# Attention on one core: which of two waits ACT's exponential carries, and which stands alone in front of it

## Chip, cores and metric

One core of a Trainium2 chip. The metric is the device time of one execution in microseconds, the median of several runs. TensorE is called PE here, VectorE DVE, ScalarE ACT, GpSimd POOL; SP issues the DMAs.

## What is computed

Two transformer layers over 4096 tokens of width 256, in fp32. Each layer has attention with 16 heads of 16 columns, then a feed-forward part, with residuals and layer norms. Layer 0 is causal; layer 1 is not. The part that the change touches, cut from the reference:

```python
# layer 0
scores = jnp.einsum('bhqd,bhkd->bhqk', q, k) / jnp.sqrt(jnp.float32(HEAD_DIM))
causal = jnp.tril(jnp.ones((t, t), dtype=bool))
scores = jnp.where(causal[None, None], scores, -jnp.inf)
attn = jax.nn.softmax(scores, axis=-1)
out = jnp.einsum('bhqk,bhkd->bhqd', attn, v)
# layer 1: the same without the mask
weights = jax.nn.softmax(scores, axis=-1)
out = jnp.einsum('bhqk,bhkd->bhqd', weights, V)
```

## The kernel before

The program runs in stages with a barrier between them: projections of layer 0, attention of layer 0, feed-forward, projections of layer 1, attention of layer 1, output projection, and a last network. Only `attention` matters here; it is called for both layers.

**Tiling.** The 16 heads are four groups of four (`GH = 4`). A unit is one group and one block of 512 queries (`QB`), so there are 32 units in a layer. In a unit the keys run in tiles of 128: always 32 tiles in layer 1, and 32, 28, 24, ... 4 in layer 0, whose units of a group go from the last block of queries to the first. That makes 1024 key tiles in layer 1 and 576 in layer 0, 1600 in all. A key tile has four score matmuls, one a head: 128 keys by 512 queries each.

**The order of work.** `order(u)` writes out a list of steps for each unit, and PE, ACT and DVE each walk through the same list and take their own part of each step:

- `score`: PE multiplies K and Q into one of three PSUM banks (line 839), ACT takes the exponential of that bank into `att_probs` (line 898). The bank is then free.
- `max`: PE makes scores of the next unit (line 801) in one of two pairs of banks, DVE reduces them to maxima (line 915). The maxima are needed before the next unit starts. One such item stands behind every second score where there are enough of them; the last unit of a layer has none.
- `values`: PE multiplies `att_probs` of a key tile by V (line 864), in two halves of 256 queries, two key tiles behind the scores (`LAG = 2`). Each half has one matmul a head, four in all in different columns of the array.
- once a unit: `turn_max` (the maxima of the next unit turned, copied at line 879 and put into Q by a DMA), `keep_out` (line 908) and `turn_out` (PE at line 873, ACT's copy at line 903, then DVE's division at lines 952 and 956).

In a row, a key tile on PE is: score of head 0, of head 1, a maxima item, values (first half), score of head 2, of head 3, a maxima item, values (second half). PE waits for nothing but what its next instruction needs, but takes its queue in order.

**The waits.** `scored` is counted up by PE once a `score`, `turn_max` or `turn_out` (the steps in `RING`), `emptied` by ACT when it has read the bank. Both count in the order of the ring, so PE's score number n waits until the exponential of number n-3 has ended. `values_done` is counted up by PE after the second half of a key tile's values. `att_probs` has room for four key tiles (`PBUFS = 4`), so the exponential of head 0 of tile k waits for the values of tile k-4; for heads 1 to 3 of a tile only the score is waited for. `out_read` is DVE's, one a unit, and the copy at line 903 waits for it beside `scored`.

**Two waits in front of one instruction.** An instruction of these engines carries one wait here. Where `wait_ge` is called twice ahead of an instruction, the built program has the wait that was called first on the instruction itself, and the one called last in an EVENT_SEMAPHORE instruction of its own in front of it, on ACT's queue (named with the line of its `wait_ge`). It takes its place in the order: what is behind it isn't looked at before it is met. In the kernel before, that is line 894, the wait for `scored`.

Of the kernel before, what the change touches and what calls it, by code (L numbers as in the profile page):

```python
# [533 lines left out]
def attention(nc, core, ps, ident, layer, causal, q_parts, k_parts, v_dram, K, o_all):  # L534
# [51 lines left out]
    def order(u):  # L586
        nk, nxt, todo = keys(u), u + 1, hosted[u]
        slots = nk * GH
        last = max([n for n, (w, _) in enumerate(todo) if w == nxt], default=-1)
        near_end = slots - (SEAM if nk > QT else SEAM - 2)  # L590
        cost = [max_width(*item) + 64 for item in todo]
# [47 lines left out]
    def width(u, kt):  # L639
        return max(0, kt - (keys(u) - QT)) * P if causal else 0  # L640

    plan = [order(u) for u in range(UNITS)]
    RING = ("score", "turn_max", "turn_out")
# [20 lines left out]
    def column(h):  # L664
        b, j = half_of(h)
        return b * PAIRS + j

    with ExitStack() as ctx:
# [21 lines left out]
        scored = core.sem(pre + "scored")  # L690
# [15 lines left out]
        with nc.Block() as block:  # L706
            if causal:
                @block.gpsimd
                def _(pool):
                    pool.memset(band[:], 0.0).then_inc(ones_set, 1)  # L710
                    pool.memset(pick[:], 0.0).then_inc(ones_set, 1)
                    pool.wait_ge(ones_set, 2)
                    for b in range(2):
                        rows = slice(b * HALF, (b + 1) * HALF)
                        for m in range(2):

                            pool.affine_select(out=pick[rows, m], in_=pick[rows, m], compare_op=ALU.not_equal, fill=1.0,
                                               base=m * HALF, pattern=[[-1, P]], channel_multiplier=1).then_inc(ones_set, 1)
                            pool.affine_select(out=band[rows, m], in_=band[rows, m], compare_op=ALU.is_ge, fill=MASKED,
                                               base=m * HALF, pattern=[[-1, P]], channel_multiplier=1).then_inc(ones_set, 1)  # L720
                    pool.wait_ge(ones_set, 10)
                    for u in range(UNITS):
                        for kt in range(keys(u) - QT, keys(u)):
                            pool.wait_ge(emptied, last_score(u, kt) + 4)
                            square = probs[:, (n_key[u] + kt) % PBUFS, :, width(u, kt):width(u, kt) + P]
                            pool.affine_select(out=square, in_=square, compare_op=ALU.is_ge, fill=0.0, base=0,  # L726
                                               pattern=[[0, GH], [1, P]], channel_multiplier=-1).then_inc(masked, 1)
# [60 lines left out]
            def _(pe):  # L788
# [36 lines left out]
                for u in range(UNITS):  # L825
# [4 lines left out]
                    for step, at in zip(plan[u], place[u]):  # L830
                        what = step[0]
                        if what in RING:
                            pe.wait_ge(emptied, at + 1)
                        if what == "score":
                            _, kt, h = step
                            b, j = half_of(h)
                            lo = width(u, kt)
# [38 lines left out]
            @block.scalar  # L876
            def _(act):
                def keep_turned(par, at):
                    act.activation(negT[:, par, :], ring(at)[0:PARTS * NEG, 0:P], ACT.Copy).then_inc(emptied, 1)  # L879

                act.sem_inc(emptied, 2)
                act.sem_inc(out_kept, 1)
                act.wait_ge(scored, 1)
                keep_turned(0, -1)
                for u in range(UNITS):
                    for step, at in zip(plan[u], place[u]):
                        what = step[0]
                        if what == "score" and step[2] == 0:

                            act.wait_ge(values_done, n_key[u] + step[1] + 1)  # L890
                        if what == "turn_out":
                            act.wait_ge(out_read, step[1] + 1)
                        if what in RING:
                            act.wait_ge(scored, at + 2)
                        if what == "score":
                            _, kt, h = step
                            lo = width(u, kt)
                            act.activation(probs[:, (n_key[u] + kt) % PBUFS, column(h), lo:QB], ring(at)[:, lo:QB], ACT.Exp,  # L898
                                           scale=SCALE).then_inc(emptied, 1)
                        elif what == "turn_max":  # L900
                            keep_turned((u + 1) % 2, at)
                        elif what == "turn_out":
                            act.activation(out[:].rearrange("p t h e -> p (t h e)"), ring(at), ACT.Copy).then_inc(emptied, 1)  # L903
                        elif what == "keep_out":
                            v = step[1]
                            act.wait_ge(values_done, n_key[v + 1] + PBUFS)

                            act.activation(outT[:], ps[:, 6, :], ACT.Copy).then_inc(out_kept, 1)
# [897 lines left out]
```

## Time and profile before

| | |
|---|---|
| median of 3 runs | 5400.65 us (5383.06 to 5416.19) |
| the profiled execution's own time | 5378.21 us |
| its span, first to last instruction | 5375.6 us |
| instructions | 101793 |
| mean granted TensorE clock | 0.941 |
| layer 0's exponentials, first and last start | 284.4 and 1833.3 us |
| layer 1's exponentials, first and last start | 2520.5 and 5093.0 us |

The profile is one execution. Its engine rows count an instruction as busy from its start to its end; a matmul's end is modelled, and a matmul can begin while the one before it is still in the array, so that PE's busy share says little about what it could still take. In the timeline a row merges instructions of one kind that follow each other: start, time from the first's start to the last's end, count, and in brackets how long the engine had been idle and what ended that. PEld is PE's weight load, which runs beside the matmuls.

### The profile page before, as it was taken

Reading aid. Unit: us, or ns where it says so; the run is one execution under the profiler, and the core shown is the slowest. Engines: PE = TensorE matmul, PEld = TensorE weight load, DVE = VectorE, ACT = ScalarE, POOL = GpSimd, SP = SyncE. Lnnn points to the kernel's source line nnn. Section 1 sums busy time; section 2 is a strip of 40 time slices with the busy share of each in tenths; the row PEclk is TensorE's granted clock in tenths of the full one; section 3 lists DMA queues with packets and bytes.
Section 4 is the critical chain, followed back from the end, with each engine's and each line's share of the span. In section 5 each row is a group of like instructions: output and inputs, shape, how many; then the busy total and the mean of one; then the engine's idle time right before and its main releaser. Section 6 shows DMA issues by size and latency. Waiting matters only on the chain. (4 is left out here: it accounts for less than half of the span.)

```text
span 5375.6 us, 101793 instructions
## 1 busy us (share of the span) xinstructions
PE 5017.1 (93%) x42036; PEld 2053.1 (38%) x42036; DVE 4509.5 (84%) x5080; ACT 3777.9 (70%) x7189; POOL 316.1 (6%) x482
## 2 busy tenths in 40 slices
PE   7699999999999678876999999999999999999998
PEld 4333433433333245542333333333333333333343
DVE  3678889889876479948999999999999999999356
ACT  2177788788777422232888888888888888888853
POOL 3200000000000011130000000000000000000030
PEclk7589999999998789995999999999999999999999
DMA  4301010010000000052100001000010000000000
GB/s 130 105 22 27 11 30 20 14 39 11 11 7 7 20 16 12 6 182 55 42 4 8 5 5 42 8 5 5 5 42 8 5 4 8 8 5 5 9 1 32
DMA packets 138201, 131.30 MB, mean 24 GB/s; under 512 B 61802, under 2 KB 96490, under 8 KB 137706
## 3 DMA queue, kind: packets, MB, share of 16 engines
q1 hardware_dynamic: 137738, 124.80, 8.2%
q8 instruction: 331, 5.42, 0.4%
q14 instruction: 132, 1.08, 0.1%
HBM read 76.75 MB, written 46.66 MB: 23 GB/s over the span
## 5 line engine op out<-in xcount | busy, mean ns | idle before, releaser
L915 DVE TENSOR_REDUCE att_mx<-ps 128x2 f32<-128x1024 f32 (+2 forms) x3200 | 3757.9, 1192 | 304.4 <-PE ps L801 205.2
L898 ACT ACTIVATE att_probs<-ps 128x512 f32<-128x512 f32 (+3 forms) x6400 | 3386.3, 583 | 648.2 <-PE ps L839 559.8
L864 PE MATMUL ps<-att_probs,att_V 128*17 128x256 f32 (+1 forms) x25088 | 1970.5, 389 | 0.2
L839 PE MATMUL ps<-att_Q,K 50*128 50x512 f32 (+3 forms) x6400 | 1732.5, 495 | 49.9 <-ACT att_probs L898 28.8
L801 PE MATMUL ps<-K,att_Q 48*128 48x512 f32 (+2 forms) x6400 | 1429.0, 415 | 91.3 <-DVE att_mx L915 54.9
L839 PEld LDWEIGHTS ps<-att_Q,K 50*128 50x128 f32 x6400 | 686.8, 186 | 1417.0 <-ACT att_probs L898 1262.9
L864 PEld LDWEIGHTS ps<-att_probs,att_V 128*17 128x17 f32 x25088 | 426.2, 96 | 1071.5 <-issue 605.9
L801 PEld LDWEIGHTS ps<-K,att_Q 48*128 48x128 f32 x6400 | 679.6, 194 | 173.2 <-DVE att_mx L915 121.9
L726 POOL TENSOR_SCALAR_AFFINE_SELECT att_probs<-att_probs 128x512 f32<-128x512 f32 x128 | 81.6, 637 | 1551.4 <-ACT att_probs L898 1551.4
L1169 PE MATMUL ps<-wguT,mlp_xqT 128*128 128x512 f32 (+1 forms) x384 | 161.5, 571 | 0.5 <-DVE mlp_h L1277 0.2
L1368 POOL MEMSET mix_power<- 128x1 f32 x1 | 0.1, 99 | 2682.3 <-POOLq L131 2682.3
L952 DVE RECIPROCAL att_rden<-att_out 128x16 f32<-128x16 f32 x64 | 16.2, 254 | 161.3 <-ACT att_out L903 161.3
L879 ACT ACTIVATE att_negT<-ps 32x128 fp32r<-32x128 f32 x64 | 16.1, 251 | 184.4 <-PE ps L811 184.4
L1208 ACT ACTIVATE mlp_gate<-ps 128x704 f32<-128x704 f32 x32 | 24.2, 757 | 141.6 <-PE ps L1169 141.6
L483 DVE TENSOR_TENSOR proj_qprod<-ps,proj_tabT 128x1024 f32<-128x1024 f32 x32 | 38.4, 1220 | 83.5 <-PE ps L329 83.5
L1169 PEld LDWEIGHTS ps<-wguT,mlp_xqT 128*128 128x128 f32 x384 | 72.6, 196 | 73.9 <-issue 65.3
L1187 PE MATMUL ps<-wdT,mlp_hqT 128*128 128x256 f32 (+1 forms) x384 | 96.0, 392 | 1.1 <-DVE mlp_y L1256 1.1
L1607 PE MATMUL ps<-xT_all,net_w 128*128 128x512 f32 x192 | 95.1, 618 | 0.0
L392 ACT ACTIVATE proj_xT<-ps 128x512 f32<-128x512 f32 x32 | 17.6, 595 | 109.9 <-PE ps L311 109.9
L1555 DVE TENSOR_SCALAR cn_cf<-cn_th,cn_ab 128x512 f32<-128x512 f32 x24 | 13.1, 546 | 83.6 <-ACT cn_th L1689 83.0
L1187 PEld LDWEIGHTS ps<-wdT,mlp_hqT 128*128 128x128 f32 (+1 forms) x384 | 71.2, 192 | 27.2 <-issue 12.4
L791 PE MATMUL ps<-att_band,att_pick 64*128 64x128 bf16 x1024 | 81.5, 228 | 0.0
(207 smaller groups left out, 2385.6 us busy)
## 6 DMA issues: line engine op xcount, KB each, us to landing
att_Q<-qhi_scratch SPq DMA_DIRECT2D x256, 64.0 KB, 2.3
K<-khi_scratch SPq DMA_DIRECT2D x256, 64.0 KB, 2.3
v_scratch<-proj_vpad SPq DMA_DIRECT2D x16, 544.0 KB, 3.4
att_V<-v_scratch SPq DMA_DIRECT2D x64, 136.0 KB, 2.5
att_Q<-qlo_scratch SPq DMA_DIRECT2D x128, 64.0 KB, 2.3
K<-klo_scratch SPq DMA_DIRECT2D x128, 64.0 KB, 2.3
proj_x<-in_L_attn_x SPq DMA_DIRECT2D x8, 512.0 KB, 5.1
qhi_scratch<-proj_qhipart SPq DMA_DIRECT2D x16, 256.0 KB, 3.0
```

What stands on the lines that cost most here:

```text
L483: dve.tensor_tensor(prod[name][:, m], of[name], tabT[:, j % 2, m, :].unsqueeze(1).to_broadcast([P, 2, B]), ALU.mult).then_inc(prods[name], 1)
L726: pool.affine_select(out=square, in_=square, compare_op=ALU.is_ge, fill=0.0, base=0, pattern=[[0, GH], [1, P]], channel_multiplier=-1).the ...
L791: return pe.matmul(dst, pick[rows, m], band[rows, m], start=False, stop=(m == 1))
L801: mm = pe.matmul(bank(b)[:, 0:wide], Q[rows, slot_of(u), j, qt * P:(qt + 1) * P], K[rows, par_of(u), j, c * QB:c * QB + wide], start=True, ...
L839: mm = pe.matmul(ring(at)[:, lo:QB], K[rows, par_of(u), j, kt * P:(kt + 1) * P], Q[rows, slot_of(u), j, lo:QB], start=True, stop=True)
L864: mm = pe.matmul(ps[VW * h:VW * h + HV, 6, lo:(part + 1) * (QB // 2)], V[:, par_of(v), kt, HV * h:HV * (h + 1)], probs[:, (n_key[v] + kt) ...
L898: act.activation(probs[:, (n_key[u] + kt) % PBUFS, column(h), lo:QB], ring(at)[:, lo:QB], ACT.Exp, scale=SCALE).then_inc(emptied, 1)
L915: dve.tensor_reduce(mx[:, min(u % NQB, 1), :, j, qt, c], ps[:, 2 + 2 * pair:4 + 2 * pair, 0:max_width(u, i) // 2], AX.X, ALU.max).then_inc ...
L1169: mm = pe.matmul(gu_ps[:, b:to], xqT[:, par, c, :], wguT[:, c, b:to], start=(c == 0), stop=(c == DC - 1))
L1187: mm = pe.matmul(down, hqT[0:kw, par, k, :], wdT[0:kw, k, :], start=(k == 0), stop=(k == NK - 1))
L1208: act.activation(gate[:], gate_ps, ACT.Silu).then_inc(s["gate_kept"], 1)
L1607: mm = pe.matmul(bank1(k, m), nets.w1[:, c, m * P:(m + 1) * P], xT_all[:, c, cols_of(k)], start=(c == 0), stop=(c == DC - 1))
```

## The change

In ACT's walk through the steps, the wait for `scored` is called ahead of the waits for `values_done` and `out_read`, not behind them.

```diff
@@ -885,13 +885,13 @@
                 for u in range(UNITS):
                     for step, at in zip(plan[u], place[u]):
                         what = step[0]
+                        if what in RING:
+                            act.wait_ge(scored, at + 2)
                         if what == "score" and step[2] == 0:
 
                             act.wait_ge(values_done, n_key[u] + step[1] + 1)
                         if what == "turn_out":
                             act.wait_ge(out_read, step[1] + 1)
-                        if what in RING:
-                            act.wait_ge(scored, at + 2)
                         if what == "score":
                             _, kt, h = step
                             lo = width(u, kt)
```

What the built programs have on ACT at the end of a unit and the start of the next, in layer 0, before. A row is one kind of instruction in a row; in brackets are the semaphores it waits for, in order, the last of two being the one that it carries. Semaphores are used again from stage to stage and are printed by their first name: `proj0_q_lo_made` is `scored`, `proj0_q_hi_stored` is `values_done`, `proj0_k_lo_stored` is `out_read`.

```order
L898 ACTIVATE att_probs<-ps 128x512 [waits proj0_q_lo_made,proj0_q_hi_stored]
L898 ACTIVATE att_probs<-ps 128x512 [waits proj0_q_lo_made] x3
L898 ACTIVATE att_probs<-ps 128x512 [waits proj0_q_lo_made,proj0_q_hi_stored]
L908 ACTIVATE att_outT<-ps 128x512 [waits proj0_q_hi_stored]
L898 ACTIVATE att_probs<-ps 128x512 [waits proj0_q_lo_made] x3
L898 ACTIVATE att_probs<-ps 128x512 [waits proj0_q_lo_made,proj0_q_hi_stored]
L898 ACTIVATE att_probs<-ps 128x512 [waits proj0_q_lo_made] x3
L903 ACTIVATE att_out<-ps 128x512 [waits proj0_q_lo_made,proj0_k_lo_stored]
L898 ACTIVATE att_probs<-ps 128x512 [waits proj0_q_lo_made,proj0_q_hi_stored]
```

And the same place after, on ACT:

```order
L898 ACTIVATE att_probs<-ps 128x512 [waits proj0_q_hi_stored,proj0_q_lo_made]
L908 ACTIVATE att_outT<-ps 128x512 [waits proj0_q_hi_stored]
L898 ACTIVATE att_probs<-ps 128x512 [waits proj0_q_lo_made] x3
L898 ACTIVATE att_probs<-ps 128x512 [waits proj0_q_hi_stored,proj0_q_lo_made]
L898 ACTIVATE att_probs<-ps 128x512 [waits proj0_q_lo_made] x3
L903 ACTIVATE att_out<-ps 128x512 [waits proj0_k_lo_stored,proj0_q_lo_made]
L898 ACTIVATE att_probs<-ps 128x512 [waits proj0_q_hi_stored,proj0_q_lo_made]
```

No activation has moved. In the rows with two waits, one in four exponentials and the copy at line 903, the two have changed places. The orders of PE, DVE, POOL and SP are the same in both programs.

## Rows read from the trace of the kernel before

**Rows 1.** The page: span, busy us, share and instructions of each engine.

```profile
span 5375.6 us, 101793 instructions
...
PE 5017.1 (93%) x42036; PEld 2053.1 (38%) x42036; DVE 4509.5 (84%) x5080; ACT 3777.9 (70%) x7189; POOL 316.1 (6%) x482
```

**Rows 2.** Busy us (instructions) of PE, PEld, DVE, ACT, POOL by stretch, then clock.

```profile
400.00:1600.00 1200.00, 1164.89 (x11342) 466.25 (x11343) 1023.41 (x1021) 935.50 (x1880) 63.71 (x100) 0.97 0.07 19
2575.00:5015.00 2440.00, 2431.80 (x23396) 888.25 (x23396) 2389.06 (x2089) 2135.93 (x3965) 0.00 (x0) 1.00 0.04 12
5020.00:5093.00 73.00, 72.34 (x652) 26.80 (x648) 0.68 (x2) 67.37 (x131) 0.00 (x0) 1.00 0.01 1
```

**Rows 3.** Who waited for whom, whole run: us, times, longest.

```profile
ACT att_probs L898 <- PE ps L839: 559.8, 1693, 4.9
```

**Rows 4.** Timeline, layer 1: start, length, engine, line, count, [idle before].

```profile
4000.49 0.63 PE L864 MATMUL ps<-att_probs,att_V 128*17 128x256 f32 x8
...
4001.05 0.50 PE L839 MATMUL ps<-att_Q,K 50*128 50x512 f32 x2
...
4001.64 2.25 ACT L898 ACTIVATE att_probs<-ps 128x512 f32<-128x512 f32 x4 [0.22 <-PE ps L839]
...
4001.72 0.63 PE L864 MATMUL ps<-att_probs,att_V 128*17 128x256 f32 x8
...
4002.27 0.52 PE L839 MATMUL ps<-att_Q,K 50*128 50x512 f32 x2
...
4003.52 0.50 PE L839 MATMUL ps<-att_Q,K 50*128 50x512 f32 x2
...
4004.11 2.25 ACT L898 ACTIVATE att_probs<-ps 128x512 f32<-128x512 f32 x4 [0.22 <-PE ps L839]
```

**Rows 5.** Groups by line, 2700 to 4300: count, busy us, mean ns, idle.

```profile
L915 DVE TENSOR_REDUCE att_mx<-ps 128x2 f32<-128x1024 f32 x1273 | 1546.9, 1225 | 17.0 <-PE ps L801 8.7
L898 ACT ACTIVATE att_probs<-ps 128x512 f32<-128x512 f32 x2543 | 1383.5, 596 | 191.8 <-PE ps L839 148.1
```

**Rows 6.** Line 894 (durations min/median/max in ns).

```profile
L894 ACTq EVENT_SEMAPHORE  x1664: 17/17/17, 284.3 to 5096.5; - x185
```

**Rows 7.** Timeline, layer 0, around two pairs of scores.

```profile
1003.88 0.50 PE L839 MATMUL ps<-att_Q,K 50*128 50x512 f32 x2
...
1004.47 1.09 ACT L898 ACTIVATE att_probs<-ps 128x512 f32<-128x512 f32 x2 [0.32 <-PE ps L839]
...
1005.23 0.50 PE L839 MATMUL ps<-att_Q,K 50*128 50x512 f32 x2
...
1005.77 1.09 ACT L898 ACTIVATE att_probs<-ps 128x512 f32<-128x512 f32 x2 [0.21 <-PE ps L839]
```

**Rows 8.** Timeline of ACT, layer 0, the copy at line 903.

```profile
902.60 0.60 ACT L903 ACTIVATE att_out<-ps 128x512 f32<-128x512 f32 x1 [0.39 <-PE ps L873]
903.09 1.08 ACT L898 ACTIVATE att_probs<-ps 128x512 f32<-128x512 f32 x2
```

**Rows 9.** Timeline of PE, layer 1, first and last small slip.

```profile
2533.96 0.51 PE L839 MATMUL ps<-att_Q,K 50*128 50x512 f32 x2
...
5012.00 0.52 PE L839 MATMUL ps<-att_Q,K 50*128 50x512 f32 x2
```

**Rows 10.** Timeline, layer 1's last unit.

```profile
5062.05 0.49 PE L839 MATMUL ps<-att_Q,K 50*128 50x512 f32 x2
...
5062.64 2.06 ACT L898 ACTIVATE att_probs<-ps 128x512 f32<-128x512 f32 x4 [0.16 <-PE ps L839]
...
5063.03 0.75 PE L839 MATMUL ps<-att_Q,K 50*128 50x512 f32 x2
```

**Rows 11.** Timeline of PE, layer 0.

```profile
303.73 0.75 PE L839 MATMUL ps<-att_Q,K 50*128 50x512 f32 x2
...
1746.19 0.52 PE L839 MATMUL ps<-att_Q,K 50*128 50x512 f32 x2
```

**Rows 12.** Timeline of DVE, layer 0.

```profile
593.53 18.62 DVE L915 TENSOR_REDUCE att_mx<-ps 128x2 f32<-128x1024 f32 x16
```

## The prediction

> **What bounds the kernel now.** The page's first lines come first [rows 1]: PE 93% busy, DVE 84%, ACT 70%. These are averages over stages, so the second view is busy time by stretch [rows 2]. Layer 1's attention without its last unit (2575 to 5015) has PE at 2432 of 2440 us, DVE at 2389 (98%) and ACT at 2136 (88%); its last unit (5020 to 5093) has PE at 72.3 of 73, ACT at 67.4 and DVE at nothing; layer 0's attention (400 to 1600) has PE at 97%, DVE at 85% and ACT at 78%. By shares, DVE and PE could both be the bound of layer 1. Third, the longest waits [rows 3]: the exponentials wait for the score matmuls (559.8 us, 1693 times). A busy PE can hide lost time, because the ends of its matmuls are modelled and overlap, so the last view is the order in time.
>
> Layer 1 repeats one pattern [rows 4]. Call the score matmuls of one key tile s0 to s3 and their exponentials e0 to e3. PE issues s0 and s1 together (4001.05), two maxima matmuls, eight value matmuls (4001.72), then s2 and s3 (4002.27), maxima, values, and s0 again at 4003.52. From s0 to s2 it takes 1.22 us, from s2 to the next s0 1.25 us. The difference is in one place: the pair s0, s1 lasts 0.50 us, so both start together, while s2, s3 lasts 0.52, so s3 starts about 0.02 late. Scores go through a ring of three banks, so s3 needs e0's bank: e0 starts at 4001.64 and takes 0.60 [rows 4, 5], ends at 4002.24, and s3 starts at 4002.27 + 0.02 = 4002.29, some 0.05 after it. Everything behind s3 on PE's in-order queue is then 0.02 late. s1 waits in the same way for e2, but is not late.
>
> **Why e0 is late.** L894's wait for the scores stands as an instruction of its own in front of 1664 activations (1600 e0 and 64 copies at L903), each taking 17 ns [rows 6]. In time order [rows 7], from the start of the scores to the start of the exponential takes 0.59 us for e0 (1003.88 to 1004.47; in rows 4, 4001.05 to 4001.64; in rows 10, 5062.05 to 5062.64), but 0.54 for e2, which carries its wait (1005.23 to 1005.77). So the handover through a separate instruction costs 0.05 to 0.06 us. That this instruction costs nothing while ACT works is seen where e0 follows the L903 copy [rows 8]: 902.60 and 903.09 are 0.49 apart with the copy 0.60 long, as between e0 and e1 in rows 7 (two in 1.09).
>
> **The change, part by part.** It moves no work: PE, DVE, POOL and SP keep their order, and ACT has as many instructions. On e0 it swaps the two waits: the separate one is now for the value matmuls, four tiles back, and e0 carries the one for its score.
>
> (1) The separate wait. What it waits for is the second half of the values of tile k-4, which PE issues in tile k-2: for the tile whose s0 starts at 4003.52 that is the group at 4000.49, over by 4001.12 [rows 4]. e0 of that tile starts at 4004.11, and e3 in front of it is the last quarter of the block at 4001.64. So the wait has long been met when ACT gets to it, and e3's 0.60 us covers the instruction; 0.22 us of idle time follow even then. Cost taken: nothing. If the cover failed, it would be the 0.06 us of today, paid on the other wait. Queued behind the wait are e0 to e3 and, through the ring, s3.
>
> (2) e0 starts 0.055 us sooner after its score. Bounds for one tile: 0 (PE has other work) and 0.06 (everything behind is released by e0). In layer 1 the saving is cut at 0.02, because s3 then meets the values in front of it, not e0. s1 behind e2 is not late even now; with the change both halves look like s0's, 1.22 each.
>
> (3) The copy at L903 carries its score wait too. It comes once a unit; the e0 behind it moves with it, and that is in the count below.
>
> Count by tiles, from the pair s2, s3 and the end of e0, over all 1600 tiles. Where s3 starts 0.05 us after e0's end it waits for e0.
> - Layer 1, 31 units of 32 tiles: 887 tiles slip by 0.02 to 0.03 (first at 2533.96, last at 5012.00 [rows 9]): 887 x 0.02 = 18 us. 73 slip by more than 0.06 (unit starts, slots without a maxima item): 73 x 0.055 = 4 us. The other 32 do not wait for e0.
> - Last unit, 32 tiles without maxima [rows 10]: the pair s2, s3 lasts 0.75, a slip of 0.26. The circle is e0, s3, values, s0, e0, with nothing beside it on PE, and all 0.055 come out of it: 32 x 0.055 = 2 us.
> - Layer 0, 576 tiles: 221 have the small slip (last pair at 1746.19 [rows 11]): 221 x 0.02 = 4 us. 153 have one over 0.06, the first of those with a steady pattern at 303.73 (0.75 for the pair [rows 11]): 153 x 0.055 = 8 us. In 202 s3 does not wait for e0: nothing.
>
> Sum: 18 + 4 + 2 + 4 + 8 = 36 us. The least by these rows is 0; the most is 1600 x 0.06 = 96 us, if no tile were cut at 0.02. I take 36, since the steady 1.22 of the half tile that waits for nothing stands in all of layer 1.
>
> **Is DVE the floor?** It matters: two reductions are in each layer-1 tile, 2 x 1.225 = 2.45 us [rows 5] of 2.46 to 2.47 (4001.64 to 4004.11 in rows 4). But in layer 0, sixteen of them stand in 18.62 us [rows 12], so (18.62 - 1.22) / 15 = 1.16 us apart, at 1.22 each: a reduction starts before the last one has ended. Two in a tile need 2.32, and DVE has 0.14 to spare. The idle time that DVE is given in layer 1 is put down to PE [rows 5]. The Trainium skill, "VectorE: DVE Perf Modes", section "The DRAIN you can't avoid", says that the next operation does not start until the pipe is empty, with an exception for operations that are not held; by its first half layer 1 would have almost no room, and the trace does not agree for these reductions (1.16 against 1.22).
>
> **Against the runs shown.** The profiled execution took 5378.21 us (span 5375.6): 5378.2 - 36 = 5342 on its own scale. The median of the runs is 5400.65, 22 higher and spread over 33 us; the same 36 us off it gives 5364.
>
> **Rivals.**
> A. DVE sets layer 1's period after all. Then the 18 us fall away, since a shorter PE pattern only makes PE wait for the reductions: 4 + 2 + 4 + 8 = 18 us off, 5383. For it: 98% busy. Against it: rows 12. Chance 0.12. By the page's rule the room would be 0.01 to 0.02 a tile, 9 to 18 us of the 18.
> B. More than the slip comes back: PE's 1.22 is not a floor in layer 1, or in layer 0 e0's lead goes on to reductions and masks in the units that end with idle PE. If every second tile gave 0.055 and not its slip, 1600 / 2 x 0.055 = 44 us, plus half of the 36: about 62 us, 5339. For it: ACT's 559.8 us of waiting [rows 3] is far above what I count. Against: most of it lies beside a PE that works. Chance 0.12.
> C. The change does nothing that shows: e0 starts at 0.59 whatever carries the wait, because it is the first after idle time. 5401. Against: e2 too starts after idle time, at 0.54 (rows 7: 0.21 idle). Chance 0.06.
> D. Slower: the values are what comes last. If e0 was released by the value matmuls, then the instruction that carried that wait was right before, and now ACT's queue stands at it and pays 0.055 after it, with e0 to e3 and PE's ring behind: by the same count +36 us, 5437, and at most +96. It decides from the point where the values of tile k-4 end after s0 of tile k, which is 3 us later than now. The time order puts the values' end 3 us ahead of e0 (part 1), and rows 3 put the exponentials' waits on the scores' line L839. Chance 0.03.
> The forecast, with its sum within 25 to 48 us: 0.67.
>
> **How the numbers follow.** What a measurement of this kernel can tell from no change is about 1%, 54 us. The forecast's 36 us is 0.67%. Of its 0.67 I put 0.05 over 1% for the spread of the runs, of B 0.09: 0.14 faster. Slower by over 1% needs the upper half of D or a disturbed median: 0.03. The rest, 0.83, is within 1%. The range: 5335 (B) to 5393 (A with 10 us of the runs' spread) leaves out C, D and B's far end.
>
> **What would show it.** Right: L894's instruction is gone, one at the values' wait is in its place, 1600 + 64 as before; from s0 to e0 0.53 to 0.54 us; the pair s2, s3 at 0.50 in layer 1, its tile at 2.44 to 2.45, that stretch of rows 2 shorter by 20 us or so; DVE's share up to 99% with no longer reductions; in the last unit the pair s2, s3 at 0.69 or 0.70. Wrong: e0 still at 0.59 (C); e0 at 0.54 with the tile at 2.46 (A; then s0 to s2 grows and maxima matmuls wait for att_mx); exponentials whose wait ends with L864 (D). A granted clock in layer 0 away from the 0.97 of now [rows 2] would move the time for another reason: PE there falls to its lower level (1.2 GHz) in short stretches, and each 0.01 of clock over 1200 us is worth up to 12 us.

## The result: 57 us less, 1.04%, and the profile after

The changed kernel took 5319.25 us in the median (5309.70 to 5358.00), the kernel before, measured beside it, 5376.36 (5369.45 to 5416.19). The ratio is 0.9896, with an interval of 0.9874 to 0.9917. The forecast was 36 us off 5400.65, a ratio of 0.9933; what came is 57 us, and 5319 lies below the range's low end of 5335. Part of that distance is the starting value: the kernel before ran 24 us lower in this comparison than in the three runs that the prediction had. The ratio itself, put on 5400.65, gives 5344. But the interval does not hold the forecast's 0.9933, so something is missing from the sum. One of the seven executions of E5, an experiment below, took 7206 us at a granted clock of 0.55 and is left out of its figures.

The profiled execution took 5309.70 us. The page's head, against [rows 1]:

```profile
span 5307.5 us, 101793 instructions
...
PE 4955.1 (93%) x42036; PEld 2017.7 (38%) x42036; DVE 4498.3 (85%) x5080; ACT 3777.1 (71%) x7189; POOL 315.1 (6%) x482
```

As many instructions on each engine, 68 us less. PE's busy time fell by 62 us although it does the same matmuls. That does not tell the cause: a late second score makes a pair's busy time longer (0.52 for 0.50), and so does a lower clock. PE's mean granted clock is 0.948, against 0.941.

Where the 68 us are is seen in the exponentials' first and last start in each layer (line, engine, count, ns min/median/max, first and last start):

```profile
L898 ACT ACTIVATE att_probs<-ps x2304: 272/594/641, 283.9 to 1793.9; 128x512 f32<-128x512 f32 x160, 128x384 f32<-128x384 f32 x20, 128x256 f32<-128x256 f32 x12
...
L898 ACT ACTIVATE att_probs<-ps x4096: 591/597/634, 2478.3 to 5025.0; 128x512 f32<-128x512 f32 x196
```

Layer 0 went from 1548.9 us (284.4 to 1833.3) to 1510.0, 38.9 less where the forecast had 12. Layer 1 went from 2572.5 (2520.5 to 5093.0) to 2546.7, 25.8 less where it had 24. The other 3 us lie between and behind the layers. So layer 1 came as forecast and layer 0 gave three times as much.

Busy time by stretch, columns as in [rows 2]: layer 0's middle, layer 1 without its last unit, and layer 0 from first to last exponential.

```profile
400.00:1600.00 1200.00, 1167.05 (x11501) 465.71 (x11501) 1033.05 (x1034) 949.51 (x1907) 63.45 (x100) 0.98 0.07 19
2530.00:4950.00 2420.00, 2413.42 (x23418) 868.51 (x23414) 2383.16 (x2090) 2138.34 (x3969) 0.00 (x0) 1.00 0.04 12
283.90:1793.90 1510.00, 1466.82 (x14305) 586.37 (x14308) 1238.91 (x1241) 1190.59 (x2396) 80.59 (x127) 0.96 0.07 18
```

And the last of these in the kernel before:

```profile
284.40:1833.30 1548.90, 1503.27 (x14305) 600.70 (x14308) 1242.94 (x1241) 1192.13 (x2396) 80.93 (x127) 0.94 0.07 18
```

In layer 1 the clock is 1.00 in both, and the time fell with it unchanged: DVE's share rose from 97.9% to 98.5%, ACT's from 87.5% to 88.4%. In layer 0 the clock rose from 0.94 to 0.96 over the whole of it. The stretch that the prediction read (400 to 1600, 0.97 then and 0.98 now) leaves out the short units at the end, where much of the low clock lies.

**The handover.** The separate instructions have moved as the built programs said: 1600 at line 892 (the values), 64 at line 894 (out_read), 17 ns each, where [rows 6] had 1664 for the scores.

```profile
L892 ACTq EVENT_SEMAPHORE  x1600: 17/17/17, 278.7 to 5022.5; - x178
...
L894 ACTq EVENT_SEMAPHORE  x64: 17/17/17, 376.4 to 5027.0; - x64
...
ACT att_probs L898 <- PE ps L839: 284.5, 565, 4.9
```

The waits for the scores are down from 559.8 us in 1693 times [rows 3] to 284.5 in 565. That row overstates the change, because a stretch of idle time of 0.15 us or less is put down to nothing. All of ACT's idle time in front of its exponentials fell from 648.2 to 596.3 us on the two pages.

The same e0 as the one at 1004.47 in [rows 7], the 1081st exponential, now starts 0.53 us after its score instead of 0.59:

```profile
996.15 0.50 PE L839 MATMUL ps<-att_Q,K 50*128 50x512 f32 x2
996.68 1.09 ACT L898 ACTIVATE att_probs<-ps 128x512 f32<-128x512 f32 x2 [0.26 <-PE ps L839]
...
3899.72 0.50 PE L839 MATMUL ps<-att_Q,K 50*128 50x512 f32 x2
...
3900.94 0.50 PE L839 MATMUL ps<-att_Q,K 50*128 50x512 f32 x2
...
3902.17 0.50 PE L839 MATMUL ps<-att_Q,K 50*128 50x512 f32 x2
...
3909.50 0.49 PE L839 MATMUL ps<-att_Q,K 50*128 50x512 f32 x1
...
5001.30 0.57 PE L839 MATMUL ps<-att_Q,K 50*128 50x512 f32 x2
...
5002.35 0.63 PE L839 MATMUL ps<-att_Q,K 50*128 50x512 f32 x2
```

In layer 1 the pairs of scores now last 0.50, one each 1.22 us, and the tile takes 2.45 (3899.72 to 3902.17, against 2.47 in [rows 4]). Of the 992 pairs s2, s3 outside the last unit, 31 still have a small slip behind e0's bank and 34 a large one, where 887 and 73 had. In the last unit the pairs last 0.57 and 0.63 where one in two lasted 0.75 [rows 10].

**DVE is not the floor.** The groups of line 915 and 898, 2700 to 4300, against [rows 5]:

```profile
L915 DVE TENSOR_REDUCE att_mx<-ps 128x2 f32<-128x1024 f32 x1283 | 1553.7, 1225 | 9.4 <-PE ps L801 8.6
L898 ACT ACTIVATE att_probs<-ps 128x512 f32<-128x512 f32 x2565 | 1395.3, 596 | 180.4 <-PE ps L839 21.4
```

Ten more reductions fit into the same 1600 us, each as long as before, and DVE's idle time fell from 17.0 to 9.4 us. The 1283 reductions are busy for 1553.7 us together, 1211 ns for each at 1225 ns long, so they still overlap. From 3899.72 to 3909.50 in the timeline above are eight half tiles: 9.78 / 4 = 2.445 us a tile, just under two reductions of 1225 ns.

### The profile page after: what moved, and what is told of

Same layout as the page of the kernel before. It is cut to its first block and busy times, and to the rows that moved or that the text cites. A ratio compares the mean times of both kernels' runs of the same rounds, so it can differ in the third digit from the quotient of the medians.

```text
span 5307.5 us, 101793 instructions
## 1 busy us (share of the span) xinstructions
PE 4955.1 (93%) x42036; PEld 2017.7 (38%) x42036; DVE 4498.3 (85%) x5080; ACT 3777.1 (71%) x7189; POOL 315.1 (6%) x482
## 5 line engine op out<-in xcount | busy, mean ns | idle before, releaser
L898 ACT ACTIVATE att_probs<-ps 128x512 f32<-128x512 f32 (+3 forms) x6400 | 3385.5, 583 | 596.3 <-PE ps L839 284.5
L839 PE MATMUL ps<-att_Q,K 50*128 50x512 f32 (+3 forms) x6400 | 1686.9, 492 | 43.9 <-ACT att_probs L898 21.0
L801 PE MATMUL ps<-K,att_Q 48*128 48x512 f32 (+2 forms) x6400 | 1397.3, 414 | 91.7 <-DVE att_mx L915 54.7
L839 PEld LDWEIGHTS ps<-att_Q,K 50*128 50x128 f32 x6400 | 657.0, 185 | 1395.2 <-ACT att_probs L898 1269.7
L801 PEld LDWEIGHTS ps<-K,att_Q 48*128 48x128 f32 x6400 | 651.1, 192 | 173.6 <-DVE att_mx L915 122.1
```

The lines of the kernel that those rows point to most:

```text
L801: mm = pe.matmul(bank(b)[:, 0:wide], Q[rows, slot_of(u), j, qt * P:(qt + 1) * P], K[rows, par_of(u), j, c * QB:c * QB + wide], start=True, ...
L839: mm = pe.matmul(ring(at)[:, lo:QB], K[rows, par_of(u), j, kt * P:(kt + 1) * P], Q[rows, slot_of(u), j, lo:QB], start=True, stop=True)
```

## The experiments

Two questions. Which parts of the gain belong to which layer and which wait? And why did layer 0 give more than the count of late scores? One theory: the direct saving there is bigger than counted. The other: PE's clock fell to its lower level less often, because PE stands still less at the starts of units. All ratios are to the kernel before, run beside them.

### E1, the kernel before once more

No edit; it gives the scatter, and a second profile.

> The kernel before, unchanged, for the granted clock of each of its executions. The changed kernel's profile shows layer 0's attention 38 us shorter, where the prediction had 12. Theory C (clock): the rest is TensorE's granted clock there, so this kernel's executions scatter with their clock, 4 to 6 us for each 0.001, its mean clock is 0.940 to 0.942 against 0.946 for the changed one, and at the same clock the two kernels lie 35 to 45 us apart. Theory L (latency): the handover of 0.06 us comes back more often in layer 0 than counted; then at the same clock they lie 55 to 65 us apart and the clocks do not differ by more than 0.001.

Measured: 5393.72 us, ratio 1.0003 (0.9990 to 1.0016). Its runs' clocks lie between 0.936 and 0.942, and the time goes with them: a straight line through these 12 runs gives 3.7 us for each 0.001, one through all 61 runs of this kernel with the experiments 4.1; 3.9 is used below. (0.001 of clock over 5380 us is 10.8 us more at the lower of the two levels, half speed, so one such microsecond costs about 0.36.)

The expectation asked how far apart the two kernels lie at the same clock. By the line through the 61 runs, the 14 runs of the changed kernel (the nine above and E8) lie 45 us below it, 35 to 51 each. That is the upper end of theory C's 35 to 45, well under theory L's 55 to 65. Their mean clock is 0.9442, against 0.9404 in the 49 runs of the kernel before that stand beside the experiments; theory C had asked for 0.946.

The profile shows the clock's price in one unit. Layer 0 has units of 32 tiles; one of them, in E1:

```profile
1052.60:1140.70 88.10, 87.64 (x784) 33.51 (x783) 72.13 (x68) 68.08 (x132) 2.47 (x4) 0.90 0.02 6
...
1040.00:1048.00 8.00, 6.72 (x65) 3.43 (x69) 6.45 (x10) 5.27 (x14) 1.33 (x3) 0.94 0.06 18
...
1056.00:1064.00 8.00, 8.00 (x44) 3.29 (x40) 5.54 (x5) 4.63 (x9) 0.00 (x0) 0.50 0.02 8
```

and the same unit in the first profile of the kernel before:

```profile
1055.30:1136.70 81.40, 80.07 (x784) 31.07 (x783) 71.52 (x68) 67.89 (x132) 2.50 (x4) 1.00 0.02 6
...
1056.00:1064.00 8.00, 7.24 (x64) 3.10 (x64) 6.89 (x8) 7.10 (x15) 0.00 (x0) 1.00 0.17 49
```

The same 784 matmuls take 6.7 us longer. Its clock of 0.90 means 2 x 0.10 x 88.1 = 17.6 us at 1.2 GHz, so 0.38 us lost for each. In the eight microseconds at 0.50, PE is busy all the time and gets 44 matmuls done, not 64. What it did before the clock fell was the last tiles of the unit before, which get narrower down to 128 queries, with the turn of the maxima: PE is 84% busy there in E1 (6.72 of 8 us from 1040 to 1048). The clock fell at this turn of units in the first profile too:

```profile
1046.00:1054.00 8.00, 7.39 (x55) 3.47 (x59) 2.28 (x5) 4.12 (x12) 1.27 (x2) 0.50 0.02 5
```

There it was back at its upper level when the unit of 32 tiles began, at 1055.3. So both executions lost the clock at the same turn of units and got it back at different times.

### E2 and E3, the change in one layer only

```diff
+                        if causal and what in RING:        # E3: not causal
+                            act.wait_ge(scored, at + 2)
...
-                        if what in RING:
+                        if not causal and what in RING:    # E3: causal
                             act.wait_ge(scored, at + 2)
```

> The change in layer 0's attention alone. Both theories: layer 1's tile stays at 2.465 us. Theory C: 12 us from the handover and about 20 from the clock in layer 0, so 25 to 38 us faster than before, with a granted clock of 0.944 to 0.946. If the clock of the changed kernel's profile was luck and not the change: 10 to 15 us faster, clock 0.941. Theory L: 25 to 38 us faster with the clock of before.

> The change in layer 1's attention alone. By the steps of the prediction 24 us faster (22 us in 31 units, 2 us in the last one), the layer-1 tile at 2.445 us, layer 0 and its clock as before (0.940 to 0.942). If the clock rises through anything that shortens the program, this one rises too (0.944 or more) and it is 40 us or more faster.

Measured: E2 5363.74 us, ratio 0.9949 (0.9936 to 0.9961); E3 5370.13, ratio 0.9952 (0.9934 to 0.9971). The product is 0.9901, against 0.9896 for both together: the parts add up. The mean clock of the runs was 0.9436 in E2 and 0.9389 in E3, against 0.9395 in the kernel before beside them. So the clock goes up with the change in layer 0 and not with the change in layer 1, which saved as much time (25.8 us in the profile after). Set against the line of E1, E2 lies 12 us below it and E3 31, 43 together: of E2's gain over half came with the clock, of E3's nothing. Layer 0 from first to last exponential, E2:

```profile
284.70:1809.20 1524.50, 1482.79 (x14305) 592.15 (x14308) 1238.53 (x1241) 1190.51 (x2395) 80.59 (x127) 0.95 0.07 18
```

and E3:

```profile
288.40:1851.70 1563.30, 1517.57 (x14305) 605.80 (x14308) 1243.81 (x1241) 1191.50 (x2396) 80.60 (x127) 0.93 0.07 17
```

A single profile says little about the clock: E3 runs the same layer 0 as the kernel before and took 14 us longer in it. The means over the runs carry the comparison.

### E4, no separate wait for the values at all

Leaves out the wait for the value matmuls of four tiles ago; the wait for the score stays, and it covers that one, since PE makes those values before that score.

```diff
-                        if what == "score" and step[2] == 0:
-
-                            act.wait_ge(values_done, n_key[u] + step[1] + 1)
```

> The changed kernel without the separate wait for the value matmuls: PE issues the values of tile k-4 before the score of tile k, so the wait for the score covers it. It tells whether the separate instruction costs anything where it now stands. Prediction's part 1: nothing, within 3 us of the changed kernel (5310 to 5325), layer-1 tile 2.446. Rival: it still costs part of its 0.06 us in layer 0, where exponentials follow closely; then 5 to 15 us faster than the changed kernel.

Measured: 5322.56 us, ratio 0.9885 (0.9868 to 0.9903). The changed kernel gave 0.9896 (0.9874 to 0.9917), and 0.9893 (0.9873 to 0.9914) in E8. These intervals are some 10 us wide to each side, too wide for the rival's 5 to 15 us. At the same clock (the line of E1) E4 lies 44 us below the kernel before and the changed kernel 45. In 15 units of layer 0 that ran at full clock in E4 and in a profile of the changed handover (after, E2, E8), E4 is 0.3 us longer over 220 tiles, not shorter. So the separate instruction with a wait that has long been met costs nothing that shows.

### E5 and E6, more work for PE in layer 0's empty slots

In layer 0, one in two score pairs has no maxima item behind it in some tiles. E5 puts two matmuls there (K by K, results never read) in the kernel before, E6 in the changed one. They add 302 matmuls and take nothing away. (The expectation speaks of 174 places; there are 151.)

```diff
+                if causal and h % 2 and slot not in at:
+                    out.append(("fill", kt))
...
+                        if what == "fill":
+                            pe.wait_ge(max_taken, nxt + 1)
+                            for b in range(2):
...
+                                pe.matmul(ps[:, 2 + 2 * (nxt % 2) + b, :], K[rows, par_of(u), 0, 0:P],
+                                          K[rows, par_of(u), 0, 0:QB], start=True, stop=True)
```

> The kernel before, and in layer 0's attention, where no maxima item follows a pair of scores, one pair of matmuls of K with K into the free maxima banks, whose result nobody reads. The handover of 0.06 us stays as it is. It asks whether a fuller PE alone raises the granted clock. Theory C: yes, layer 0 spends fewer microseconds at the lower level (under 150 us, before 180), the clock is 0.943 or more and the time falls by 8 to 25 us, at 4 us for each 0.001. Theory L, or clock as luck: the clock stays at 0.939 to 0.940 and the time stays or rises by up to 10 us, as PE has 174 pairs more to do.

> The changed kernel with the same filler. Theory C: clock above that of the changed kernel (0.946 or more) and 0 to 15 us faster than it. Otherwise: clock the same, 0 to 10 us slower than it.

Measured: E5 5355.22 us, ratio 0.9951 (0.9931 to 0.9971); E6 5296.64, ratio 0.9836 (0.9814 to 0.9857). By the medians the filler is worth 31 us in both, E5 against the kernel before beside it (5386.66) and E6 against E8 (5327.97). By E5's ratio it is 26 us there, with an interval of 16 to 37. E6 is faster than both kernels. Layer 0 in E5:

```profile
284.10:1807.60 1523.50, 1484.94 (x14603) 594.18 (x14601) 1241.21 (x1241) 1196.19 (x2396) 80.85 (x127) 0.97 0.07 18
```

and in E6:

```profile
284.40:1780.30 1495.90, 1463.64 (x14603) 582.83 (x14601) 1236.56 (x1241) 1196.53 (x2395) 80.85 (x127) 0.98 0.07 18
```

E5 saves as much in layer 0 as E2 does (1523.5 and 1524.5 of 1548.9) with every e0 still late and 298 more PE instructions recorded. The runs' mean clock is 0.9502 in E5 and 0.9530 in E6, against 0.9402 and 0.9438 (E8) without the filler. Layer 0's time at the lower level, summed over stretches of 25 us as 2 x (1 - clock) x length, is 180 us before, 209 in E3, 149 in E2, 106 in the changed kernel, 78 in E5 and 51 in E6.

The filler's own time hardly shows at the place of [rows 11]. E6, where L849 makes the scores and L841 is the filler:

```profile
303.05 0.50 PE L849 MATMUL ps<-att_Q,K 50*128 50x512 f32 x2
303.38 0.40 PE L841 MATMUL ps<-K 48*128 48x512 f32 x2
...
304.27 0.50 PE L849 MATMUL ps<-att_Q,K 50*128 50x512 f32 x2
...
305.49 0.50 PE L849 MATMUL ps<-att_Q,K 50*128 50x512 f32 x2
```

The kernel before:

```profile
302.74 0.50 PE L839 MATMUL ps<-att_Q,K 50*128 50x512 f32 x2
...
305.20 0.49 PE L839 MATMUL ps<-att_Q,K 50*128 50x512 f32 x2
```

From the first pair to the third it is 2.44 us with the filler and 2.46 without, where E6 has the new handover too. Without the filler, the pair at 303.73 comes 0.23 sooner and its second score then waits for e0's bank.

Whole units tell more. Take the units of layer 0 that ran at full clock throughout, with the filler and without. In E5 they are 14, with 268 tiles and 60 of the 302 fillers: together 0.06 us shorter than in the kernel before (before, E1, E3). In E6 they are 19, with 300 tiles and 98 fillers: 1.9 us longer than with the changed handover alone (after, E2, E8). So, as far as these units show, the filler saves nothing where the clock is full, and its gain comes with the clock. By the line of E1 its matmuls also cost something: E5 lies 8 us above that line, and E6 40 us below it where the changed kernel lies 45, at clocks of 0.950 to 0.953 where the line (0.934 to 0.946) has no run of its own.

### E7 and E9, the separate wait at other exponentials

E7 is the kernel before, with a wait for the values also called ahead of e2's wait for its score, so that e2 too has its score's wait in an instruction of its own (the trace has 3264 of them at line 894, and 0.59 us from score to e2). E9 is the changed kernel with the old order at e2, and the new one left at e0. E7:

```diff
-                        if what == "score" and step[2] == 0:
+                        if what == "score" and step[2] in (0, 2):
```

and E9:

```diff
+                        if what == "score" and step[2] == 2:
+                            act.wait_ge(values_done, n_key[u] + step[1] + 1)
                         if what in RING:
```

> The kernel before with the suspected cost twice in a tile: e2 too carries a wait for the value matmuls (long met), and its score wait stands alone in front. By the steps of the prediction s1 then waits for e2 as s3 does for e0: 0.02 us more in each layer-1 tile (2.465 to 2.485), 17 to 22 us in layer 1; in layer 0 12 to 20 us, and by theory C some more through the clock. In all 25 to 60 us slower than before. If e0's lateness is not passed on through the ring, nothing.

> The changed kernel with the handover moved from e0 to e2: e0 carries its score wait, e2 carries the wait for the values and its score wait stands alone. E7 cost nothing, and the explanation to be tested is that a late s3 (by e0) and a late s1 (by e2) are the same 0.02 us: s3's slip pushes the next s0 and so gives s1 the time that a late e2 takes. Then the layer-1 tile here goes back to 2.465 us, with the slip now in the pair s0, s1, and this kernel is 17 to 22 us slower in layer 1 than the changed one, about 30 to 50 in all, some 10 to 25 us faster than before. If instead e2's lateness has no price at all, the tile stays at 2.446 and the time at the changed kernel's.

Measured: E7 5387.27 us, ratio 1.0001 (0.9984 to 1.0019); E9 5368.88, ratio 0.9972 (0.9954 to 0.9990). For E7 the expectation was wrong. Its timeline in layer 1:

```profile
4018.30 0.50 PE L839 MATMUL ps<-att_Q,K 50*128 50x512 f32 x2
...
4019.52 0.52 PE L839 MATMUL ps<-att_Q,K 50*128 50x512 f32 x2
...
4020.77 0.50 PE L839 MATMUL ps<-att_Q,K 50*128 50x512 f32 x2
...
4021.36 2.30 ACT L898 ACTIVATE att_probs<-ps 128x512 f32<-128x512 f32 x4 [0.16 <-PE ps L839]
...
4021.98 0.53 PE L839 MATMUL ps<-att_Q,K 50*128 50x512 f32 x2
```

Still one slip a tile. The reading: a late exponential frees its bank 0.59 + 0.60 + 0.05 = 1.24 us after its pair of scores began. Without a slip the next pair begins at 1.22, and its second score is 0.02 too early for the bank. But when one pair has slipped, PE is late with everything behind it, the next pair begins at 1.25 (4019.52 to 4020.77), and its second score finds the bank free. One late exponential or two, the tile is 0.02 longer. The whole of layer 1 fits this: outside the last unit, a small slip that waits for its bank stands in 540 second pairs and 388 first pairs of the 992 tiles, against 887 and none in the kernel before. The expectation had counted each handover as if it stood alone. E9's timeline shows the slip moved by half a tile:

```profile
4001.01 0.50 PE L839 MATMUL ps<-att_Q,K 50*128 50x512 f32 x2
...
4001.61 2.25 ACT L900 ACTIVATE att_probs<-ps 128x512 f32<-128x512 f32 x4 [0.23 <-PE ps L839]
...
4002.23 0.52 PE L839 MATMUL ps<-att_Q,K 50*128 50x512 f32 x2
...
4003.48 0.50 PE L839 MATMUL ps<-att_Q,K 50*128 50x512 f32 x2
```

Here 4001.01 is s2, s3 with e2 at 0.60, and the long pair is s0, s1. Tile: 2.47, as before the change; so layer 1's gain is gone (2571.3 us from first to last exponential, 2572.5 before). E9's layer 0:

```profile
283.70:1830.70 1547.00, 1507.09 (x14307) 603.49 (x14308) 1242.88 (x1241) 1192.96 (x2395) 80.61 (x127) 0.94 0.07 18
```

Its 12 units at full clock (188 tiles) are 0.014 us a tile shorter than in the kernel before, half of what the changed kernel gives there (see below); over 576 tiles that is 8 of the 15 us. The mean clock of its runs is 0.9421, against 0.9417 beside it. So with e0 on time and e2 late the clock does not rise. That speaks for a late exponential anywhere in the tile as what lowers it, and not for e0's place. Where the other 7 come from is not shown.

### E8, the changed kernel once more

> The changed kernel, unchanged, beside the others. Both theories: 55 to 75 us faster than before, clock 0.944 to 0.946, layer-1 tile 2.446.

Measured: 5327.97 us, ratio 0.9893 (0.9873 to 0.9914). The mean clock of its runs is 0.9438, of the kernel before beside it 0.9402. The result stands, and the clock is higher here too. Its profile shows what the change does in layer 0 at a low clock:

```profile
283.00:1815.80 1532.80, 1492.19 (x14306) 594.93 (x14308) 1239.84 (x1241) 1191.24 (x2396) 80.84 (x127) 0.94 0.07 18
```

By stretches of 25 us it spent 170 us at the lower level, nearly the 180 of the kernel before, and layer 0 is 16 us shorter and not 39.

### E10, e0 made later still

In the kernel before, three instructions that count up a semaphore nobody waits for are put between the wait for the score and e0. In the built program the first of the three carries that wait (the separate instruction is left at the 64 copies only), so three instructions stand in front of e0 where one stood: two more.

```diff
+        handed = core.sem(pre + "handed")
...
+                        if what == "score" and step[2] == 0:
+                            for _ in range(3):
+                                act.sem_inc(handed, 1)
```

> The kernel before with e0 made still later: behind L894's wait three increments of a semaphore that nobody waits for, two instructions more between the score and e0 in every tile. If x is what this adds to the time from s0 to e0 (0.03 to 0.12 us by the 0.06 of one), the ring has no slack left at e0 and layer 1's tile grows by all of x: 1024 x in layer 1, 300 to 576 x in layer 0. With x = 0.1 that is 130 to 160 us slower. If the 0.02 of the prediction were not e0's, the time stays.

Measured: 5659.99 us, ratio 1.0526 (1.0484 to 1.0567). Layer 1, where L840 makes the scores and L902 the exponentials:

```profile
4000.78 0.50 PE L840 MATMUL ps<-att_Q,K 50*128 50x512 f32 x2
4001.55 2.07 ACT L902 ACTIVATE att_probs<-ps 128x512 f32<-128x512 f32 x4 [0.85 <-PE ps L840]
...
4002.00 0.70 PE L840 MATMUL ps<-att_Q,K 50*128 50x512 f32 x2
...
4003.42 0.50 PE L840 MATMUL ps<-att_Q,K 50*128 50x512 f32 x2
...
4004.64 0.69 PE L840 MATMUL ps<-att_Q,K 50*128 50x512 f32 x2
```

e0 is at 0.77 instead of 0.59 (0.765 in the median), the pair s2, s3 lasts 0.70, and the tile takes 2.64: the 0.17 of e0 comes out in full, as s3 now waits for e0's bank alone. That is 0.086 us for each of the two instructions added. The prediction's circle is right, and below 0.59 it is PE's own work that cuts the saving at 0.02. Layer 0:

```profile
284.60:1948.40 1663.80, 1609.97 (x14305) 661.03 (x14308) 1251.48 (x1241) 1168.71 (x2395) 80.62 (x127) 0.91 0.06 16
```

It is 115 us longer than the kernel before's, with a clock of 0.91 and 307 us at the lower level, 127 more than before. At 0.36 us each these are 46 of the 115: the clock falls with a later e0, so the link holds in both directions.

## Why the prediction was too small, point by point

**(1) The separate wait for the values costs nothing.** Right, by E4.

**(2) e0 0.055 sooner, cut at 0.02 in layer 1.** Right. From score to e0 it is 0.53 us in the median for 0.59, 0.060 less where the prediction had 0.055; the pair s2, s3 lasts 0.50, the tile 2.445 to 2.45; layer 1 gave 25.8 us for the 22 + 2 of the sum. E10 shows the circle uncut, E9 that it is the handover and not its place.

**The last unit.** A tile takes 2.17 us there in the median, for 2.23 before, 2 us less in all, as the sum had it. The pair was to be at 0.69 or 0.70. In the profile after it is at 0.57 to 0.63 in the rows shown, with the waiting spread over both halves; in E8, the same program, it is where the prediction put it:

```profile
5019.60 0.51 PE L839 MATMUL ps<-att_Q,K 50*128 50x512 f32 x2
...
5020.59 0.69 PE L839 MATMUL ps<-att_Q,K 50*128 50x512 f32 x2
```

**DVE as the floor (rival A).** It fell: the tile is under two reductions' 2.45 us, DVE's idle time still falls. The first half of the Trainium skill's rule that the prediction weighed ("VectorE: DVE Perf Modes", section "The DRAIN you can't avoid") does not hold for these reductions in the trace after either: one for each 1211 ns, at 1225 ns long.

**Rivals C and D.** Both fell: e0 moved, and the values' wait is never the last (E4).

**Rival B.** Its time of 62 us off is near the 57, but for layer 1 its reason did not hold: PE's 1.22 is the floor. For layer 0, see below.

**The step that failed is layer 0's term, 4 + 8 = 12 us.** It was wrong in two ways.

First, the direct part is some 16 us. Units at full clock in both profiles show it without the clock. One of 32 tiles, before:

```profile
1437.60:1518.70 81.10, 79.75 (x786) 30.89 (x785) 71.53 (x68) 68.00 (x132) 2.53 (x4) 1.00 0.03 7
```

and the same after:

```profile
1420.80:1501.00 80.20, 79.08 (x784) 30.51 (x783) 71.24 (x68) 67.97 (x132) 2.45 (x4) 1.00 0.03 7
```

0.9 us for 32 tiles, 0.028 a tile where the sum had 12 / 576 = 0.021. By that, 576 x 0.028 = 16 us. Other units agree: 14 of them, with 252 tiles, ran at full clock in at least one of the profiles before, E1 and E3 and in one of after, E2 and E8, and there a tile is 0.030 us shorter.

The same 252 tiles tell which sizes were wrong, when they are sorted by the classes of the prediction's count. The classes themselves are right: the trace has the 221, 153 and 202 tiles that it names.

| class | price in the sum | tiles measured | shorter by, us a tile |
|---|---|---|---|
| small slip | 0.02 | 103 | 0.026 |
| slip over 0.06 | 0.055 | 59 | 0.068 |
| s3 does not wait for e0 | 0 | 90 | 0.0065 |

With these prices the count gives 221 x 0.026 + 153 x 0.068 + 202 x 0.0065 = 17 us for 12. So every class was priced too low. Why a tile can give more than e0's 0.060, or something where s3 does not wait, is not shown.

Second, and larger, the granted clock. The sum was made at a fixed clock; the prediction named the clock as something that would move the time "for another reason" and gave it no term and no chance. Over all runs with the experiments it was 0.9404 in the kernel before (49 runs), and in the changed kernel, with E8, 0.9442 (14 runs). That is 2 x 0.0038 x 5380 = 41 us less at 1.2 GHz, at 0.36 us each 15 us. The whole account is then 25.8 (layer 1) + 16 + 15 = 57 us, for 57 measured; so close a fit is partly luck, since the mean clock of the kernel before alone was 0.9395 beside E1 to E4 and 0.9417 beside E9 and E10, 9 us by the same price, and the clocks of its runs in the main comparison are not on record. A second way that uses no single unit agrees: at the same clock the changed kernel is 45 us faster (E1), for 25.8 in layer 1, 16 in layer 0 and 3 outside both. The profiled execution of the changed kernel was one with a high clock (0.948), so its layer 0 shows more than a typical run, 38.9 us: 16 direct, and 74 us less at the lower level (180 to 106), 27 by the same price, together 4 more than there is.

That the clock follows from the late exponentials in layer 0, and is not chance, rests on E2 against E3 (clock up only with the change in layer 0), on E4 and E8 (0.9442 and 0.9438, the clock up again), on E5 and E6 (clock up and 31 us less with more work for PE) and on E10 (clock down with a later e0). E9 sets a limit: with e2 alone late, the clock stays where it was. That PE's standing still at the starts of units is the link, as the theory had it, is argued: E5 and E6 show that filling its gaps raises the clock, not which gaps count. The Trainium skill, "TensorE: Matmul & The Clock Gate", "Part 1: The HAM clock gate", says that the clock depends on how busy the engine has been of late, with two levels; the traces agree (0.50 and 1.00, the fall behind a stretch with PE at 84%). It puts the penalty of the ramp to full clock at under 1% of a typical kernel's span and advises against fitting a count of slow matmuls. That is said of the ramp at the start; in this kernel the clock falls again and again, some 630 of 5376 us ran at the lower level (2 x 0.059 x 5376), and the clock made about a quarter of a gain of 1.04%.

Not settled: why the same program has a clock of 0.936 in one run and 0.942 in the next, and at which unit starts it falls; no experiment took this apart.

## What to carry to other kernels

Of two waits in front of an instruction, let the one that comes last be carried by the instruction, and leave the one long met to the separate instruction: it costs nothing there, and 0.06 us if it is the late one. Count what such a handover costs only where the next engine has no other work in front of it; elsewhere a second late handover costs nothing on top of the first (E7). When PE idles in gaps, put the granted clock into the sum as a term: take the price of a microsecond at the lower level from the same unit at both levels, and try useless matmuls in PE's empty slots, which were worth 31 us by the medians here. Compare runs at the same clock, by a line of time against clock, before giving a gain to a mechanism: one profile at a high clock showed 38.9 us in layer 0 where another of the same program showed 16 (E8).

## What the runs showed of the hardware

- A wait in an instruction of its own makes the activation behind it start 0.06 us later after its releaser (0.59 against 0.53), though the instruction is recorded with 17 ns. With three instructions in front of the activation, semaphore increments of which the first carries the wait, it is 0.77 us: 0.086 for each of the two added (E10).
- 302 matmuls added to PE made the kernel 31 us faster by the medians, twice (E5 and E6), with a mean clock of 0.9502 for 0.9402 in the one and of 0.9530 for 0.9438 in the other.
- Between runs of one program the mean clock moved by 0.006 (E1) and the time by 23 us with it, some 3.9 us for each 0.001.
- Each microsecond at the lower level cost 0.36 to 0.38 us (the runs of E1; one unit at both levels in two profiles of the kernel before).
